# Forward scans through a PSUM bank: where a bidirectional recurrence adds its own terms

## What is computed

```
ek = exp(min(k, 30));  ekv = ek * v                    (v is k here)
nf, df = forward scans   a = a * decay + ekv,  b = b * decay + ek
nb, db = the same scans, backward in time
euk = exp(min(u + k, 30))
num = nf + nb - ekv + euk * v
den = df + db - ek + euk
out = sigmoid(r) * (num / max(den, 1e-8)) * (0.8 + 0.2 * tf)
```

## Time and profile before

| | us |
|---|---|
| median of 3 runs | 1259.64 (1255.48 to 1259.96) |
| the profiled execution | 1258.88 |
| its span | 1256.8 |
| VectorE busy | 683.8 (54%) |
| GpSimd busy | 311.5 (25%) |
| ScalarE busy | 526.4 (42%) |
| TensorE busy | 1047.8 (83%) |

### The profile page before, as it was taken

The page is one execution under the profiler, slowest core; times in us unless marked ns, Lnnn a source line. Parts: engine busy times, 40 slices in busy tenths (PEclk is TensorE's granted clock), DMA queues, the critical chain, the costliest instruction groups (busy, mean ns, idle before and its releaser), DMA issues.

```text
span 1256.8 us, 16771 instructions
## 1 busy us (share of the span) xinstructions
PE 1047.8 (83%) x5058; PEld 829.5 (66%) x5059; DVE 683.8 (54%) x1016; ACT 526.4 (42%) x882; POOL 311.5 (25%) x251
## 2 busy tenths in 40 slices
PE   1136789788699539999999999899897996999994
PEld 0022345345356439998999899799786885988883
DVE  6989899899854313334333333345454343334553
ACT  5454637737544313333333333344444332333453
POOL 3776728547530420002000200010202002000202
PEclk9998988898899659999999999999998998999997
DMA  4250330221021351116112721343634235111721
GB/s 185 101 161 34 127 120 34 67 73 62 0 102 68 125 181 67 67 67 148 69 67 86 180 85 67 114 107 132 193 126 142 77 123 143 67 67 67 195 83 20
DMA packets 63420, 125.53 MB, mean 100 GB/s; under 512 B 4726, under 2 KB 4762, under 8 KB 63384
## 3 DMA queue, kind: packets, MB, share of 16 engines
q1 hardware_dynamic: 54728, 107.91, 24.7%
q0 software_dynamic: 8656, 17.13, 6.7%
HBM read 93.04 MB, written 35.22 MB: 102 GB/s over the span
## 4 chain that ended last, share of the span: by engine, by line
PE 57%; issue 4%; ACT 1%; POOL 0%; DVE 0%; DVEq 0%; ACTq 0%; POOLq 0%
PE ps_h L1112 10%; PE ps_h L1113 9%; PE ps_h L1114 9%; PE ps_y L1123 9%; PE ps_y L1124 9%; PE ps_y L1125 9%; PE ps_t L1086 1%; POOL out_dram L1065 0%; ACT xh L1222 0%; ACT y L1229 0%; ACT w1h L1194 0%; DVE w1l L1245 0%; DVEq L1167 0%; DVE hl L1284 0%; ACTq L1167 0%
## 5 line engine op out<-in xcount | busy, mean ns | idle before, releaser
L1112 PE MATMUL ps_h<-xh,w1h 128*128 128x320 f32 (+3 forms) x768 | 251.1, 327 | 39.6 <-issue 37.7
L1113 PE MATMUL ps_h<-xl,w1h 128*128 128x320 f32 (+3 forms) x768 | 246.6, 321 | 0.0
L1114 PE MATMUL ps_h<-xh,w1l 128*128 128x320 f32 (+3 forms) x768 | 246.5, 321 | 0.0
L1065 POOL DMA_INDIRECT out_dram<-y,token x40 | 63.1, 1579 | 697.5 <-ACT y L1229 517.1
L1284 DVE SCALAR_TENSOR_TENSOR hl<-ps_h,hh 128x320 fp32r<-128x320 f32 (+1 forms) x192 | 107.0, 558 | 231.6 <-ACT hh L1218 226.8
L1123 PE MATMUL ps_y<-w2h,hh 128*128 128x512 f32 (+1 forms) x528 | 207.0, 392 | 1.0 <-DVE hl L1284 1.0
L1218 ACT ACTIVATE hh<-ps_h 128x320 fp32r<-128x320 f32 (+1 forms) x192 | 94.3, 491 | 269.7 <-PE ps_h L1114 269.5
L1124 PE MATMUL ps_y<-w2h,hl 128*128 128x512 f32 (+1 forms) x528 | 207.0, 392 | 0.0
L1125 PE MATMUL ps_y<-w2l,hh 128*128 128x512 f32 (+1 forms) x528 | 206.2, 391 | 0.0
L1248 DVE TENSOR_TENSOR w2l<-raw,w2h 128x512 fp32r<-128x512 f32 x128 | 88.6, 692 | 196.8 <-ACT w2h L1197 196.8
L1112 PEld LDWEIGHTS ps_h<-xh,w1h 128*128 128x128 f32 x768 | 148.2, 193 | 48.8 <-issue 39.8
(11 more groups left out here) (197 smaller groups left out, 1281.9 us busy)
## 6 DMA issues: line engine op xcount, KB each, us to landing
raw<-in_L_ffn_w_dram SPq DMA_DIRECT2D x64, 1024.0 KB, 7.2
slots<-r_rows SPq DMA_DIRECT2D x8, 1302.5 KB, 15.3
rows<-slots SPq DMA_DIRECT2D x8, 1302.5 KB, 8.9
f_rows<-in_fside_BxSxS_dram SPq DMA_DIRECT2D x5, 1024.0 KB, 5.3
rows<-in_x_dram SPq DMA_DIRECT2D x4, 1024.0 KB, 6.2
out_dram<-x_rows SPq DMA_DIRECT2D x4, 1024.0 KB, 4.7
slots<-r_rows POOLq DMA_DIRECT2D x1, 1302.5 KB, 6.8
rows<-slots SPq DMA_DIRECT2D x5, 260.5 KB, 3.6
```

What stands on the lines that cost most here:

```text
L1112: nc.tensor.matmul(o, w1h[:, j, dt, :], xh[:, dt, lo:hi], start=(dt == 0), stop=False)
L1113: nc.tensor.matmul(o, w1h[:, j, dt, :], xl[:, dt, lo:hi], start=False, stop=False)
L1114: last = nc.tensor.matmul(o, w1l[:, j, dt, :], xh[:, dt, lo:hi], start=False, stop=(dt == CT - 1))
```

## The change

The four forward scans of a unit no longer write in place. Each writes the PSUM bank ps_acc over all 512 elements, beginning from carry_in, which is the first element times decay / (1 - decay squared) (d_inv, made once). The own term is then added out of the bank on VectorE: for a denominator back into the bank, from which the maximum writes it to sums (and gives s_den, now once for each c); for a numerator straight into sums (s_num). All scans share the one bank, so each waits for the last reader before it. GpSimd's newton loses its adds. Whoever waited for s_den to find buffers free waits for both numerators now; the first reciprocal waits for the denominator of its own c. The two ratios of a unit are one instruction, but for the last unit of a batch, and have one buffer, ratios. ps_mm gives up one of three banks; tile k waits for the copy of tile k - 2, and the back projection's first bank is ps_to.

```diff
             u, r = b * CT + ct, ct % 2
-            steps = Steps(dve, s_fold, 5 * u)
-            dve.wait_ge(s_bwd, 2 * u + 2)
-            first = sums[r][:, :, :, 0]
-            steps.do(v.tensor_tensor(first, first, inv_pair[:, bass.ds(b * CT + ct, 1)].rearrange("p b c o -> p (b c) o")
-                                     .to_broadcast([P, 2, 2]), ALU.mult))
+            steps = Steps(dve, s_fold, 8 * u)
             for c in range(2):
-                for n in (1, 0):
-                    s = sums[r][:, c, n]
-                    ins = v.tensor_tensor_scan(s[:, 1:T], d0(b, c, ct, T - 1), s[:, 1:T], s[:, 0:1], ALU.mult, ALU.add)
-                    if n == 1:
-                        steps.mark(ins)
-            steps.wait()
+                dve.wait_ge(s_bwd, 2 * u + c + 1)
+                steps.mark(v.tensor_scalar(carry_in[:, c], sums[r][:, c, :, 0], d_inv[:, col(b, c, ct)], None, ALU.mult))
             dve.wait_ge(s_euk, u + 1)
+            dve.wait_ge(s_eukv, u + 1)
             for c in range(2):
-                steps.mark(v.tensor_tensor(sums[r][:, c, 1], sums[r][:, c, 1], euk[:, r, c], ALU.add))
-            steps.wait()
-            for c in range(2):
-                last = v.tensor_scalar(sums[r][:, c, 1], sums[r][:, c, 1], den_min[:, col(b, c, ct)], None, ALU.max)
-            last.then_inc(s_den, 1)
-
-        def ratio(b, ct, c):
+                for n, own in ((1, euk), (0, eukv)):
+
+                    steps.wait()
+                    if n == 0:
+                        dve.wait_ge(s_den, 2 * u + c + 1)
+                    elif c == 1 or at_least(u, 1):
+                        dve.wait_ge(s_num, 2 * u + c)
+                    steps.do(v.tensor_tensor_scan(ps_acc[:], d0(b, c, ct, T), sums[r][:, c, n], carry_in[:, c, n:n + 1],
+                                                  ALU.mult, ALU.add))
+                    if n == 0:
+                        v.tensor_tensor(sums[r][:, c, n], ps_acc[:], own[:, r, c], ALU.add).then_inc(s_num, 1)
+                    else:
+                        steps.do(v.tensor_tensor(ps_acc[:], ps_acc[:], own[:, r, c], ALU.add))
+                        v.tensor_scalar(sums[r][:, c, n], ps_acc[:], den_min[:, col(b, c, ct)], None, ALU.max).then_inc(s_den, 1)
+
+        def ratio(b, ct, cs):
 
             u, r = b * CT + ct, ct % 2
-            dve.wait_ge(s_newton, 2 * u + c + 1)
+            dve.wait_ge(s_newton, 2 * u + cs.stop)
             if ct == 0 and at_least(b, 2):
 
-                dve.wait_ge(*((s_mm, 12 * (b - 1)) if c == 0 else (s_r2, b - 1)))
...
+                dve.wait_ge(s_mm, 12 * (b - 1))
+                dve.wait_ge(s_r2, b - 1)
+            v.scalar_tensor_tensor(out=ratios[:, bass.ds(b % 2, 1), cs, ct, :].rearrange("p o c t -> p (o c) t"),
+                                   in0=sums[r][:, cs, 1], scalar=2.0, in1=sums[r][:, cs, 0],
+                                   op0=ALU.subtract, op1=ALU.mult).then_inc(s_ratio, cs.stop - cs.start)
...
             r = ct % 2
-            pool.wait_ge(s_den, u + 1)
-            pool.wait_ge(s_eukv, u + 1)
             for c in range(2):
-                g.tensor_tensor(sums[r][:, c, 0], sums[r][:, c, 0], eukv[:, r, c], ALU.add).then_inc(s_own, 1)
                 pool.wait_ge(s_rec, 2 * u + c + 1)
-                pool.wait_ge(s_own, 2 * u + c + 1)
                 g.tensor_tensor(sums[r][:, c, 1], sums[r][:, c, 1], recip0[:, c], ALU.mult)
+                pool.wait_ge(s_num, 2 * u + c + 1)
                 g.tensor_tensor(sums[r][:, c, 0], sums[r][:, c, 0], recip0[:, c], ALU.mult).then_inc(s_newton, 1)
...
-            if k < 3 and at_least(b, 1):
-                pe.wait_ge(s_x2, CT * (b - 1) + (1, 3, 4)[k])
-            if k >= 3:
-                pe.wait_ge(s_z, Z_COPIES * b + k - 2)
+            if k < 2 and at_least(b, 1):
+                pe.wait_ge(s_x2, CT * (b - 1) + 3 + k)
+            if k >= 2:
+                pe.wait_ge(s_z, Z_COPIES * b + k - 1)
```

More of the change, by code:

```diff
@@ L172, in conditioning_and_routing @@
     recip0 = sb("recip0", [P, 2, T])
-    r1T = sb("r1T", [P, 2, CT, T])
-    ratio2 = sb("ratio2", [P, 2, CT, T])
+    ratios = sb("ratios", [P, 2, 2, CT, T])
+    ratio_of = lambda b, c: ratios[:, bass.ds(b % 2, 1), c].rearrange("p o n t -> p (o n) t")
     sig = sb("sig", [P, CT, T])
@@ L198, in conditioning_and_routing @@
     ps_x = ps("ps_x", [P, T])
-    ps_mm = ps("ps_mm", [P, 3, T])
-    bank = lambda e: ps_x[:] if e == 1 else ps_mm[:, (0, None, 1, 2)[e], :]
+    ps_mm = ps("ps_mm", [P, 2, T])
+    ps_acc = ps("ps_acc", [P, T])
     ps_to = ps("ps_to", [P, C])
+    bank = lambda e: (ps_to[:], ps_x[:], ps_mm[:, 0, :], ps_mm[:, 1, :])[e]
     row_bank = lambda i, banks: (ps_to, ps_x)[i % banks]
@@ L242, in gate_piece @@
         high, low = gate_parts[2 * which:2 * which + 2]
-        raw = r1T[:, (B - 1) % 2, dt, :] if which == 0 else wm[:, which, dt, :]
+        raw = ratios[:, (B - 1) % 2, 0, dt, :] if which == 0 else wm[:, which, dt, :]
         return raw, high[:, dt], low[:, dt]
@@ L430, in gate @@
                 for dt in range(CT):
-                    nc.tensor.matmul(ps_mm[:, k % 3, :], high[:, dt, column], gate_parts[0][:, dt], start=(dt == 0), stop=False)
-                    nc.tensor.matmul(ps_mm[:, k % 3, :], high[:, dt, column], gate_parts[1][:, dt], start=False, stop=False)
-                    last = nc.tensor.matmul(ps_mm[:, k % 3, :], low[:, dt, column], gate_parts[0][:, dt], start=False, stop=(dt == CT - 1))
+                    nc.tensor.matmul(ps_mm[:, k % 2, :], high[:, dt, column], gate_parts[0][:, dt], start=(dt == 0), stop=False)
+                    nc.tensor.matmul(ps_mm[:, k % 2, :], high[:, dt, column], gate_parts[1][:, dt], start=False, stop=False)
+                    last = nc.tensor.matmul(ps_mm[:, k % 2, :], low[:, dt, column], gate_parts[0][:, dt], start=False, stop=(dt == CT - 1))
                 last.then_inc(s_mm, 1)
@@ L436, in gate @@
             for dt in range(CT):
-                last = nc.tensor.matmul(ps_mm[:, k % 3, :], wm[:, m, dt, e * P:(e + 1) * P],
-                                        r1T[:, bass.ds(b % 2, 1), dt, :].rearrange("p o t -> p (o t)"),
+                last = nc.tensor.matmul(ps_mm[:, k % 2, :], wm[:, m, dt, e * P:(e + 1) * P],
+                                        ratios[:, bass.ds(b % 2, 1), 0, dt, :].rearrange("p o t -> p (o t)"),
                                         start=(dt == 0), stop=(dt == CT - 1))
@@ L611, in gate_functions @@
                     act.wait_ge(s_mm, 12 * b + k + 1)
-                    last = a.activation(z[:, e], ps_mm[:, k % 3, :], ACT.Sigmoid, bias=bias)
+                    last = a.activation(z[:, e], ps_mm[:, k % 2, :], ACT.Sigmoid, bias=bias)
                 if GATE_TILES[k][0] == 2:
@@ L857, in second_out @@
             dve.wait_ge(s_sig2, b + 1)
-            v.scalar_tensor_tensor(out=sig[:], in0=ratio2[:, bass.ds(b % 2, 1)].rearrange("p o c t -> p (o c) t"),
+            v.scalar_tensor_tensor(out=sig[:], in0=ratio_of(b, 1),
                                    scalar=neg_scale[:, bass.ds(b, 1)], in1=sig[:],
@@ L931, in step @@
                 if cond and s >= 1:
-                    ratio(b, s - 1, 0)
-                    ratio(b, s - 1, 1)
+                    ratio(b, s - 1, slice(0, 2))
             if cond:
-                ratio(b, CT - 1, 0)
+                ratio(b, CT - 1, slice(0, 1))
             if gates:
@@ L939, in step @@
                 first_out(b)
-                ratio(b, CT - 1, 1)
+                ratio(b, CT - 1, slice(1, 2))
             if tail:
```

23 lines of the change are left out of this document (9 added, 14 removed).

## The result

The changed kernel takes 1285.67 us (median of 4 runs, 1281.85 to 1289.67); the kernel before took 1259.14 us beside it (1255.48 to 1259.96). The ratio is 1.0217 (95% interval 1.0179 to 1.0255): slower by 2.2%. The profiled execution took 1281.85 us with a span of 1280.1, against 1258.88 and 1256.8: +23.0. It is the fastest of the four, so differences of medians (+26.5 here) come out larger than those of the traces; the slowest, 1289.67 us, had a granted TensorE clock of 0.934 where this one had 0.939.

A forecast was written before the change was run, and what follows sets the result against it. VectorE was taken to bound the stretch that conditions the four batches (busy 309 of 336 us). Terms 29.1 + 22.0 - 6.8 - 10.4 + 0.2 = +34.1 on 1258.88 gave 1293 us, range 1264 to 1303.

The forecast's parts named there:

- Fold: VectorE's scans, adds and maxima, each waiting for the one before through one PSUM bank: +29.1 us.
- The bounds given for scans and adds: In the fold, scans of 1.20 to 1.32 us and adds of 0.69 to 0.80 give -8 to +6 us.
- Carries: Two 128x2 multiplies before the forward scans, held by GpSimd, the second for a whole instruction: +22.0 us.
- Ratio: Two ratios merged into one 1024-element instruction at eight places in the midst of stages, with GpSimd idle: -6.8 us.
- Ends: Last denominator ready earlier, so ScalarE's chain to the gates starts 2.6 us earlier, over four stages: -10.4 us.
- Banks: Two banks for gate tiles: late tile 5 and logits hidden, first tile of the last gate step waits: +0.2 us.
- Cover: VectorE's own longer unit: In the loop, it hides the late logits; if gone, 3 to 5 us in each of two stages.
- rival 4: The banks reach VectorE: logits late in two stages by 4 us, 1301 us; chance 0.06.
- 1 and 2 (held once, not held): Carries: the pair held once, 1278 us, chance 0.17; or not held at all, 1265 us, chance 0.13.
- 3 (waits are free): Fold runs at unwaited intervals, 8.7 us a unit, 20 us less: 1273 us; chance 0.08.
- Sum: All terms of the forecast together: +34.1 us, so 1293 us; chance 0.50.

The follow-up runs named there:

- e3: Changed kernel with the numerators' own-term adds back on GpSimd and their scans in place in SBUF: 1263.89 us, ratio 1.0048.
- e1: Changed kernel with the factor of the two carries in PSUM instead of SBUF: 1264.55 us, ratio 1.0053.
- e6: Kernel before with only the two ratios of a unit merged into one operation: 1258.84 us, ratio 0.9999.
- e11: Changed kernel with the carries' factor in PSUM and the logits ahead of gate tile 5 on TensorE: 1264.95 us, ratio 1.0049.
- e9: Kernel before with two banks for the gate tiles instead of three, run again for an undisturbed profile: 1271.32 us, ratio 1.0093.
- e8: Kernel before with each fold instruction waiting for the one before it: 1267.56 us, ratio 1.0079.
- e12: Kernel before with only the factor of the first elements' 128x4 multiply moved to PSUM: 1258.60 us, ratio 0.9992.
- e4: Changed kernel with only denominators through the bank, numerators in place, their adds on GpSimd, the two kinds' scans alternating, carries' factor in PSUM: 1246.36 us, ratio 0.9910.
- e5: As e4, with the logits ahead of gate tile 5 on TensorE: 1241.96 us, ratio 0.9878.

## Why the prediction was right

1293 us was forecast, with a range of 1264 to 1303; the time is 1285.67. Slower, by the mechanisms named. The number was better than its terms: against the trace the sum is 10.8 us too high (+34.1 for +23.3), of which the carries are 6.1 and the ends 3.8; that the profiled execution is 3.8 us under the median brings the forecast within 7.3 of it.

- **Fold: forecast +29.1, measured +30.7.** Adds were 0.70 instead of 0.75 us, scans 1.29 instead of 1.26. A wait behind s_den or s_num leaves 0.10 us (59.55 + 0.75 to 60.40), where I had put 0.04 for all. That these errors cancel to 0.1 us for each unit is luck. The bounds given for scans and adds come to -7.7 and +7.0 us, not +6. That two adds on this engine are the price, e3 shows (-29.6 us of fold).
- **Carries: forecast +22.0, measured +15.9.** The mechanism is shown by e1 and by the timeline: rest of one GpSimd instruction, then a whole one. The size was off in two ways. A held pair costs 2.2 to 2.3 us and not 2.45, as I counted a carry's own 0.2 us beside the hold and most of it lies within. The first unit went the other way (2.3 for 1.5). And of the six units of the loop's stages that I took for held, four were less so (1.64, 0.40, 1.65 and 1.31 us). The trace of before had the sign of it, and I misread it: its 128x4 multiply was held (0.74 us or more) in 9 of 16 units and not in 11, and four of the other seven are such units of the loop's stages. In the one of 0.40 us, shown here in the changed kernel, GpSimd was idle: its reciprocals stood on ScalarE behind the copies of late gate tiles. So the late tiles, a loss elsewhere, took a hold away here, which no term of the sum had.

```profile
245.37 0.44 DVE L799 TENSOR_SCALAR carry_in<-sums_odd,d_inv 128x2 f32<-128x2 f32 x2
...
246.75 1.27 POOL L353 TENSOR_TENSOR sums_even<-sums_even,recip 128x512 f32<-128x512 f32 x1 [17.36 <-ACT recip L582]
```

- **Ratio: forecast -6.8, measured -7.6.** 1.22 us for 1024 elements, with 1.32 to the next scan (1.44 in the loop). The eight pairs themselves gave 6.9 us (18.0 to 11.1), the other 0.7 lie between them. That it is worth nothing alone (e6), I did not foresee; in the changed kernel the instructions that lost it again in e6 are no longer held.
- **Ends: forecast -10.4, measured -14.2.** The wait for the gates ends 6.4 us after the last fold, as forecast (161.35 to 167.79, before 9.0). Batches 2 and 3 gave 2.7 us each; batches 0 and 1 gave 4.3 and 4.6. There the rest is again GpSimd: without its adds the last Newton multiply and the products are placed otherwise, and in batch 1 the first output took 2.34 us instead of 3.35 and the multiply ahead of it 0.69 instead of 1.59. I had not gone through the instructions behind the gates' wait.
- **Banks: forecast +0.2, nothing seen (e11).** The reason held for the logits: "Cover: VectorE's own longer unit". They were done 17.6 us after the second fold (17 forecast) and wanted 20.4 after it (21). The changed kernel with three banks wasn't tried, so its whole term isn't measured. But what it costs without that cover I put at 3 to 5 us in each of two stages; it is 12 in all (e9), since I put tile 5 at 3.7 us where it takes 6.39, and followed the late copies to the logits and not to the reciprocals, GpSimd's multiplies and the fold that they land in. As a price of a bank in a kernel with holds, rival 4 was too small; in this one it didn't happen.
- **Rivals.** 1 and 2 (held once, not held): out, by the 2.11 us pair, though two units of the loop's stages went as they had it (1.31 and 0.40 us). 3 (waits are free): out, by e8. 4 (the banks reach VectorE): out here, by the trace, in which VectorE doesn't wait for the logits, and by e11. The Trainium skill, page "VectorE: DVE Perf Modes", section The DRAIN you can't avoid, has waited and unwaited copies at one time; this case's traces don't agree for scans and adds of 512 elements (0.14 us for each wait). The Trainium skill, page "SBUF — State Buffer", section Who interferes with whom, lets VectorE's mode with two ports and GpSimd block each other for a whole instruction. The 2.11 us agree with that; no trace shows the ports, only that a PSUM operand ends the hold.
- **Sum:** 30.7 + 15.9 - 7.6 - 14.2 = +24.8 to the last ratio, -1.5 behind it, which no term had: +23.3 for the spans.

## What to carry to other kernels

Where VectorE and GpSimd share a stretch, look at each VectorE instruction for a PSUM operand. In these traces one that has one was never held, and one without, however small, waited for the rest of a GpSimd instruction when it came in the midst of GpSimd's work. Taking the hold from one instruction paid only where nothing behind it could be held in its place (e1), and gave nothing where something could (e6, e12), so count on the gain only when all of a row are moved. The shared bank paid where its chain was interleaved with work that doesn't need it (e4, e5); moving an add onto the bound engine to relieve one that had room did not (e3).

## What the hardware showed that I had not expected

- A hold moves rather than goes: e12 saved 6.2 us of it and paid 5.3 elsewhere, e6 saved 5.1 and paid 3.6, with ratios of 0.9992 and 0.9999.
- A tensor_scalar over two elements from SBUF took up to 1.31 us beside GpSimd and 0.20 to 0.23 where GpSimd was idle; a tensor_tensor over two elements with a PSUM operand took 0.12 to 0.16 (e1). A scan is held too if both its inputs are in SBUF: that of the gated recurrence took 2.17 us once (e9, at 253.58) instead of 1.22.
- A scan into PSUM took 1.291 us (median) in every kernel that had one; in place it is 1.256 to 1.262 unwaited (e5) and 1.281 to 1.284 waited (e8, e3). An add from the bank into the bank is 0.673 us where another instruction stands between it and its scan (e5) and 0.700 right behind it.
